# Q and K of two attentions as two 12-bit float32 parts, two heads in the two halves of the array's rows

## What is computed

```python
def _L0_xattn_ref(query, key, value, Wq, bq, Wk, bk, Wv, bv, Wo, bo):
    q = (query @ Wq.T + bq).reshape(B, -1, HEADS, HEAD_DIM)      # B 8, 512 rows
    k = (key @ Wk.T + bk).reshape(B, -1, HEADS, HEAD_DIM)        # 1601 rows
    v = (value @ Wv.T + bv).reshape(B, -1, HEADS, HEAD_DIM)
    scores = jnp.einsum('bqhd,bkhd->bhqk', q, k) * scale
    attn = jax.nn.softmax(scores, axis=-1)
    out = jnp.einsum('bhqk,bkhd->bqhd', attn, v).reshape(B, -1, DIM)
    return out @ Wo.T + bo

x = x + _L0_xattn_ref(_layernorm(x, axis=-1), ctx_1024, ctx_1024, ...)
...
h = x + _attention(_rmsnorm(x, g1), wq, wk, wv, wo)   # causal, rotary q and k, 512 keys
y = h + _moe(_rmsnorm(h, g2), w_router, wg, wu, wd)
```

## Time and profile before

| | us |
|---|---|
| median of 3 runs | 3326.37 (3324.26 to 3327.92) |
| the profiled execution | 3328.94 |
| its span from first to last instruction | 3327.4 |
| stage of the input projections, 20 to 290 us | 270 |
| cross-attention, 290 to 1670 us | 1380 |
| projections of the self-attention, 1670 to 1919 us | 249 |
| self-attention, 1919 to 2334 us | 415 |
| the rest, 2334 us to the end | 993 |

### The profile page before, as it was taken

One profiled execution on the slowest core, in us unless ns is written; L12 is line 12 of the kernel. 1 busy time (PEld: TensorE's weight loads), 2 busy tenths in 40 slices (PEclk: granted clock), 3 DMA queues, 4 the chain that ended last, 5 costly groups with the idle time before them and its releaser, 6 DMA issues. The chain is left out here.

```text
span 3327.4 us, 54791 instructions
## 1 busy us (share of the span) xinstructions
PE 2706.5 (81%) x14654; PEld 1326.7 (40%) x14655; DVE 1767.8 (53%) x2838; ACT 1460.1 (44%) x2951; POOL 488.0 (15%) x638
## 2 busy tenths in 40 slices
PE   7996899999999999999948778888341299999980
PEld 5662232323232323233235434443231177777760
DVE  5665776767676767677346556664222022222223
ACT  2331576767676767677713335555110022222210
POOL 2444000000000000000014411110133400000006
PEclk9996899999999999999979979999665599999995
DMA  7888444444444444443045556654444211001115
GB/s 239 266 286 155 79 72 77 71 77 71 76 72 75 73 73 75 72 74 58 22 133 195 178 131 142 142 141 105 145 144 152 95 33 33 32 32 32 32 46 182
DMA packets 317615, 347.91 MB, mean 105 GB/s; under 512 B 37328, under 2 KB 262776, under 8 KB 317312
## 3 DMA queue, kind: packets, MB, share of 16 engines
q1 hardware_dynamic: 285584, 291.53, 38.6%
q0 software_dynamic: 11392, 37.76, 3.6%
q10 hardware_dynamic: 20464, 16.40, 1.6%
HBM read 206.22 MB, written 138.57 MB: 104 GB/s over the span
## 5 line engine op out<-in xcount | busy, mean ns | idle before, releaser
L727 DVE TENSOR_REDUCE att_cross_neg_max<-att_cross_ps_s 128x1 f32<-128x802 f32 x1024 | 965.6, 988 | 357.3 <-PE att_cross_ps_s L644 355.6
L798 ACT ACTIVATE att_cross_probs<-att_cross_ps_st 128x512 f32<-128x512 f32 (+1 forms) x1664 | 901.4, 599 | 401.0 <-PE att_cross_ps_st L663 388.4
L663 PE MATMUL att_cross_ps_st<-att_cross_q_pack,att_cross_k_pack 99*128 99x512 bf16 (+1 forms) x1664 | 575.3, 391 | 42.7 <-issue 33.8
L644 PE MATMUL att_cross_ps_s<-att_cross_k_pack,att_cross_q_pack 96*128 96x401 bf16 x2048 | 548.2, 351 | 70.1 <-DVE att_cross_neg_max L727 29.5
L678 PE MATMUL att_cross_ps_o<-att_cross_probs,att_cross_v_tiles 128*32 128x512 f32 (+1 forms) x3328 | 453.4, 618 | 1.0
L644 PEld LDWEIGHTS att_cross_ps_s<-att_cross_k_pack,att_cross_q_pack 96*128 96x128 bf16 x2048 | 177.1, 100 | 420.6 <-DVE att_cross_neg_max L727 204.5
L663 PEld LDWEIGHTS att_cross_ps_st<-att_cross_q_pack,att_cross_k_pack 99*128 99x128 bf16 (+1 forms) x1664 | 163.1, 100 | 421.2 <-ACT att_cross_probs L798 293.1
L727 DVE TENSOR_REDUCE att_self_neg_max<-att_self_ps_s 128x1 f32<-128x128 f32 (+3 forms) x512 | 236.5, 489 | 162.7 <-PE att_self_ps_s L647 159.7
L798 ACT ACTIVATE att_self_probs<-att_self_ps_st 128x256 f32<-128x256 f32 (+3 forms) x512 | 208.5, 441 | 156.8 <-PE att_self_ps_st L666 150.8
L1756 DVE COPY moe_hiddenT<-moe_ps_h 128x256 f32<-128x256 f32 x142 | 60.3, 424 | 297.2 <-PE moe_ps_h L1666 297.2
L644 PE MATMUL att_self_ps_s<-att_self_k_pack,att_self_q_pack 96*128 96x128 bf16 (+3 forms) x512 | 160.6, 316 | 56.4 <-DMA att_self_q_pack<-q_parts 25.1
(11 more groups left out here) (208 smaller groups left out, 2910.6 us busy)
## 6 DMA issues: line engine op xcount, KB each, us to landing
att_cross_k_pack<-k_parts SPq DMA_DIRECT2D x192, 200.1 KB, 9.5
v_rows<-in_v_pad SPq DMA_DIRECT2D x24, 1024.0 KB, 4.5
att_cross_v_tiles<-v_rows SPq DMA_DIRECT2D x32, 768.0 KB
k_parts<-in_part SPq DMA_DIRECT2D x72, 256.0 KB, 4.0
in_rows<-in_ctx_dram SPq DMA_DIRECT2D x24, 512.0 KB, 4.8
att_cross_q_pack<-q_parts SPq DMA_DIRECT2D x192, 64.0 KB, 10.0
att_self_k_pack<-k_parts SPq DMA_DIRECT2D x192, 64.0 KB, 3.2
att_self_q_pack<-q_parts SPq DMA_DIRECT2D x192, 64.0 KB, 3.6
```

Of the source, the lines that this page charges most:

```text
L644: last = nc.tensor.matmul(ps_s[bank][:, n, 0:w], qp[v.buf][0:SROWS, j, q * P:(q + 1) * P], kp[v.buf][0:SROWS, j, s:s + w], start=True, sto ...
L663: mm = nc.tensor.matmul(ps_st[bank_of_step[s]][0:rows, q0:SEQ], kp[u.buf][0:MROWS, j, t * P:t * P + rows], qp[u.buf][0:MROWS, j, q0:SEQ], ...
L727: nc.vector.tensor_reduce(nmax[v.odd][:, col, half:half + 1], ps_s[bank][:, 0:len(spans), 0:spans[0][1]], AX.XY, ALU.max, negate=True).the ...
L798: nc.scalar.activation(pr[0:rows, (u.odd * STEPS + s) % RING, q0:SEQ], ps_st[bank_of_step[s]][0:rows, q0:SEQ], ACT.Exp).then_inc(exp_done, 1)
```

## The change

The parts become two instead of three. The high part is the float32 value with its last 12 bits cleared (`HIGH_BITS`, a bitwise AND on VectorE), the low part the rest; both are stored as float32. The three pairs high·high, low·high and high·low take 48 rows, and with the three rows for the maxima 51. Of four heads, heads 0 and 2 lie in rows 0 to 50 and heads 1 and 3 in rows 64 to 114. The products read these tiles as `float32r` (FR), one matmul and one load each, with an array tile of 64 rows and 128 columns. The order of heads within a step group and of the pieces is chosen so that a piece of one half stands beside score products of the other half, and the two products of a piece are now separate entries of the order.

```diff
-K_PARTS = (0, 1, 2, 0, 1, 0)
-Q_PARTS = (0, 0, 0, 1, 1, 2)
+K_PARTS = (0, 0, 1)
+Q_PARTS = (0, 1, 0)
+HALF = P // 2
+HIGH_BITS = -(1 << 12)
...
# project_inputs, VectorE, then ScalarE, then GpSimd
-                    nc.vector.tensor_tensor(rest[st.par][:, :, 0:st.size], full[st.par][:, :, 0:st.size],
-                                            parts[st.item][0][:, :, 0:st.size], ALU.subtract).then_inc(rest_ready, 1)
+                    nc.vector.tensor_scalar(parts[st.item][0][:, :, 0:st.size].bitcast(I32),
+                                            full[st.par][:, :, 0:st.size].bitcast(I32), HIGH_BITS, None,
+                                            ALU.bitwise_and).then_inc(high_ready, 1)
...
-                        for dst in (full[st.par], parts[st.item][0]):
-                            last = nc.scalar.activation(dst[:, i, 0:st.size], ps_k[:, i, 0:st.size], ACT.Identity,
-                                                        bias=bias[:, i:i + 1], scale=scale)
+                        last = nc.scalar.activation(full[st.par][:, i, 0:st.size], ps_k[:, i, 0:st.size], ACT.Identity,
+                                                    bias=bias[:, i:i + 1], scale=scale)
...
-                    nc.gpsimd.tensor_copy(mid[:, :, 0:st.size], rest[st.par][:, :, 0:st.size]).then_inc(mid_ready, 1)
-                    pool.wait_ge(mid_ready, st.n + 1)
-                    nc.gpsimd.tensor_tensor(low[:, :, 0:st.size], rest[st.par][:, :, 0:st.size],
-                                            mid[:, :, 0:st.size], ALU.subtract).then_inc(low_ready, 1)
+                    nc.gpsimd.tensor_tensor(low[:, :, 0:st.size], full[st.par][:, :, 0:st.size],
+                                            high[:, :, 0:st.size], ALU.subtract).then_inc(low_ready, 1)
...
# attention
-        span = -(-kv // 4)
+        span = -(-kv // 8) * 2
...
+    HEADS_OF = ((0, 2, 1, 3), (1, 3, 0, 2))
+    head_of = [HEADS_OF[s // GH % 2][s % GH] for s in range(STEPS)]
+    todo = [[(j, q, h, spans[q][h]) for j in (x, x + 2) for q in range(QT) for h in range(PIECES)] for x in range(2)]
+    pieces = []
+    for k in range(NP):
+        beside_half = head_of[int(step_of[k] % STEPS)] % 2
+        pieces.append((todo[1 - beside_half] or todo[beside_half]).pop(0))
...
-        kp = [p.sb(f"k_pack{i}", [P, GH, kv], BF16) for i in range(BUFS)]
-        qp = [p.sb(f"q_pack{i}", [P, GH, SEQ], BF16) for i in range(BUFS)]
+        kp = [p.sb(f"k_pack{i}", [P, GH // 2, kv]) for i in range(BUFS)]
+        qp = [p.sb(f"q_pack{i}", [P, GH // 2, SEQ]) for i in range(BUFS)]
...
+                def set_ones(buf):
+                    for h in range(2):
+                        at = h * HALF + SROWS
+                        sp.dma_start(kp[buf][at:at + 3, :, :].rearrange("a j n -> a (j n)"),
+                                     pr[0:3, :, :].rearrange("a r n -> a (r n)")[:, 0:GH // 2 * kv])\
+                          .then_inc(kq_in[buf], 16)
...
+                def add_mask(out, h, swap, which, stop):
+                    rows = slice(h * HALF, (h + 1) * HALF)
+                    return nc.tensor.matmul(out, keep["ident_swap_b" if swap else "ident_b"][rows, :],
+                                            keep[which + ("_swap_b" if swap else "_b")][rows, 0:out.shape[-1]],
+                                            start=False, stop=stop)
...
+                    s, w = cuts[part]
+                    mm = nc.tensor.matmul(ps_s[bank][:, part, 0:w], qp[v.buf][rows, j // 2, q * P:(q + 1) * P].bitcast(FR),
+                                          kp[v.buf][rows, j // 2, s:s + w].bitcast(FR), start=True, stop=not causal)
+                    if causal:
+                        add_mask(ps_s[bank][:, part, w - P:w], h, False, "mask_q", False)
+                        mm = add_mask(ps_s[bank][:, part, w - P:w], h, True, "mask_q", True)
...
+                        return [(at + part * STEPS / NP / cuts, lambda part=part: piece(what, v, k, part))
+                                for part in range(cuts)]
...
-                        act.dma_start(qp[v.buf][SROWS:MROWS, :, :].rearrange("a j n -> a (j n)"), nm_rows[:, :])\
-                       .then_inc(m_rows_in, 16)
+                    for h in range(2):
+                        act.dma_start(qp[v.buf][h * HALF + SROWS:h * HALF + MROWS, :, :].rearrange("a j n -> a (j n)"),
+                                      nm_rows[h * n:(h + 1) * n, :]).then_inc(m_rows_in, 16)
...
# project_self: the two casts of ScalarE go, VectorE masks instead of subtracting
-                    nc.scalar.copy(parts[w][0][:, :, :], full[w][:, :, :]).then_inc(hi_ready[w], 1)
-                    nc.scalar.copy(parts[w][1][:, :, :], rest[w][:, :, :]).then_inc(mid_ready[w], 1)
+                    nc.vector.tensor_scalar(parts[w][0][:, :, :].bitcast(I32), full[w][:, :, :].bitcast(I32),
+                                            HIGH_BITS, None, ALU.bitwise_and).then_inc(hi_ready[w], 1)
```

241 lines of the change are left out of this document (126 added, 115 removed).

## The result

The changed kernel takes 3692.86 us (median of 4 runs, 3677.34 to 3723.8) where the kernel before takes 3325.32 on the same chip: a ratio of 1.1125, 95% interval 1.1069 to 1.1181. The forecast was 3332 with a range up to 3490, so the prediction was wrong, by far more than any of its terms.

What follows compares the result with a forecast made beforehand. TensorE and VectorE were taken to hold each other in the cross-attention, the maxima to pace the self-attention. 3327.4 + 6 + 3 - 2 - 2 - 3 + 4 = 3333.4 us of span, so 3332 us; range 3240 to 3490.

Steps and rivals of the forecast that it cites:

- Part 1, the halves: Cross-attention: scores and piece products run side by side, yet +0.2 us a unit, +6 us in all, bounds -19 and +31.
- the first rival: The halves don't run side by side: 42.6 us a cross-attention unit, 3480 us in all; chance 0.13.
- the coupling with VectorE: Cross-attention: TensorE and VectorE hold each other, so TensorE's gain of 1.7 us a pair of groups shrinks to 0.16.
- the exposed weight load: Cross-attention: loads not hidden at four places of a pair of groups, 0.05 us each, 0.2 us a pair.
- my second rival: Halves overlap but each is slowed by loads setting the pace: 1.4 us a unit more, 3380 us; chance 0.06.
- Part 2, the self-attention: Self-attention, where the maxima set the pace: +3 us for 32 units, bounds -19 and +29.
- The second DMA: Self-attention: the maxima's second DMA is issued 0.73 us behind the first and the next unit waits for both, +0.7.
- The doubled masks: Self-attention: one more mask product per score and piece, in both halves at once, some 1 us a unit.
- Part 3, the projections: Projections: fewer casts and writes, -2 and -2 us at their ends, 0 and -3 inside, bounds 0 to -10.
- Part 4, the starts: Starts of both attentions: first piece waits for rows of ones by DMA, +2 us each, +4, bounds 0 and +10.
- The third: VectorE becomes the only bound: 32.6 us a cross-attention unit, 3130 us; chance 0.15 with what lies between.
- The fourth: The new product streams at half the rate, 0.43 us a score: 47 us a unit, 3620 us; chance 0.06.

Runs made afterwards that it cites:

- warm: Changed kernel plus 120 extra full-height bf16 products, once, just ahead of the self-attention's first score; 3604.0 and 3667.3 us.
- filler: Changed kernel plus 24 extra full-height bf16 products at the start of every self-attention unit, ahead of the wait for the maxima; 3559.85 us, 1.069 of before.
- cut_before: Kernel before with only the places of a piece's two products changed, set apart as in the change; 3389.73 us, 1.0225 of before.
- bf16_halves: Changed kernel with both parts stored as bf16 instead of float32, halves and order kept; 3274.67 us, 0.985 of before.
- bf16_whole: Changed kernel with parts in bf16 and the two products of a piece one behind the other again; 3199.62 us, 0.965 of before.
- low_half: Changed kernel with every product in rows 0 to 50, so nothing can run side by side; 4776.23 us, 1.437 of before.
- mask128: Changed kernel with each causal mask added by one product over all 128 rows instead of two over 64; 4049.27 us, 1.221 of before.
- tall_fr: Changed kernel with its float32r products over one tall tile, 96 or 99 rows each, instead of two halves; 3545.99 us, 1.067 of before.

## Why the prediction was wrong

**The step that failed: the clock, put at no change without a reason.** The prices of both attentions were taken where the granted clock is 1.00 and carried over to a kernel whose products use other rows of the array. The column stands in the earlier trace rows, 0.94 and 0.94, and I didn't ask what holds it. The runs showed 0.83 and 0.50 in its place. That omission is some 190 us in the self-attention (31 x (18.7 - 12.5)), 87 us between the merges of the cross-attention, and a good part of the 31 us ahead of and behind them: about three quarters of the 395. No rival had it either, so no bound could reach the result. That the clock costs this is shown (warm, filler); what makes it fall is narrowed down to half-height products together with the long loads, and why these two stays open.

**Part 1, the halves.** Right: they run side by side, a score and a piece product starting within 10 ns, and the first rival (42.6 us a unit without overlap) is seen in cut_before, 41.7. Right too was the coupling with VectorE and the cut piece behind it: the idle time of 1.0 us in every second group is there, the stepped order gave 38.65 us with no load exposed and bf16_halves has 38.7, and the same stepping for whole pieces (36.8 to 37.7, expected of bf16_whole) became 37.1. Mis-sized was one term, the exposed weight load. I took 0.05 us at four places of a pair, bounds 0 and 0.09, 0.65 us a unit; measured are 2.9. The length was read well (0.185 us, between the 0.148 and 0.192 of the earlier trace rows), but its effect was not: the load shows as 0.11 us at the start of each run of products (0.29 from first to second, instead of 0.17), and inside a run it is as long as the stream, so that loads set the pace. That was my second rival, with 1.4 us a unit; on top of exposed loads of 0.1 (40.2 in the stepping) it gives 41.6, what was measured, though this sum was made only afterwards. So the +6 us is really +74 at full clock.

On the rule of the Trainium skill that I weighed, TensorE: Matmul & The Clock Gate, Part 3 (a load overlaps a product only where the row groups differ): in low_half all loads and products share their rows, a load lasts 0.33 us at the lower clock, and products still follow each other in 0.334 and 0.427 us, the bare stream of 402 and 512 columns at 1.2 GHz. The trace doesn't agree with the rule, in float32 either, where such products follow each other; where a product over all rows stands between them, a load does show (mask128).

**Part 2, the self-attention.** At full clock (warm) a unit takes 12.5 us instead of 12.0, +16 us in all against a forecast of +3, within the bounds. The single terms were less good. The second DMA, +0.7 a unit, does not show: before, the load of the first score waits for the maxima's DMA in 23 units, 23 us together, in bf16_whole in none, and in warm in 11 of 15, for 0.6 us each. So the maxima's DMA sets the pace less than before, and not more; the sign that the first score still waits for it holds in warm alone. The doubled masks are no cost to be had back but the price of keeping the halves apart (mask128). The rest is the clock.

**Part 3, the projections.** Forecast -7, measured -13: the input projections end 9.7 us earlier, twice what I took and within the bounds, the others 3.

**Part 4, the starts.** Forecast +4. From the last instruction of the stage ahead to the first score, the cross-attention went from 69 to 75 us and the self-attention from 32 to 37: +11, over the bound by 1; both run at the lower clock.

**Rivals and bounds.** The third, VectorE as the only bound, would have needed shorter waits; its idle time grew. The fourth, half the stream rate, is refuted by tall_fr: 0.23 us from a score to the next product, not 0.43. The bounds of the parts as given add up to some 3274 and 3400 us, not to 3285 and 3395; the result lies far outside of either.

## What to carry to other kernels

A matmul that leaves half of the array's rows empty is not just a lost chance: on this core, with nothing in the other half, TensorE's clock stayed at half from where it stood at the start, and a busy share of 98% didn't bring it back; and with long loads in both halves it fell at waits that the other kernels take at full clock. So before a tile is made smaller, ask what fills the rest of the array, look at the granted clock of the stretch as at a resource, and count the weight loads of both halves against the stream. With loads short enough (bf16, good here to 16 bits of Q and K rather than 24) and pieces not cut, the same idea takes 3199.62 us, 0.965 of the kernel before.

## What was unexpected of the hardware

- The same order of bf16 products ran at a granted clock of 0.94 with 96 and 99 rows and at 0.50 with 48 and 51, over 2289 us: both start at 0.50, and only the first leaves it.
- A wait of 0.96 us for VectorE was followed by a fall of the clock 16 times in the changed kernel, while waits of 0.8 to 1.0 us at the same place are followed by none in the kernel before, tall_fr and bf16_halves.
- The clock has a memory: the same units of the self-attention run at 1.00 (12.5 us) or at 0.50 (18.7 us), and after one fall stayed low for 300 us, until the end; with 24 tall products a unit it came back after each fall.
- A one-pass float32r product loads its weights in 0.185 us and streams 512 columns in 0.22 to 0.24; bf16 loads take 0.095.
- Products in the two halves start within 10 ns of each other, but with a product over all rows between them nothing lay side by side any more and the loads showed: a unit of the self-attention went from 18.7 to 30.0 us, both at 0.50.
